# Routed tiles of a mixture-of-experts layer: the spread of gathered rows moves from ScalarE's queue to SyncE's, with new distances for gathers, lists and weights

## What is computed

```python
x = x + ffn(cond(x, cond_512, ...), router_w, e_bias, gate_w, up_w, down_w, ...)   # x: (8, 1024, 512)

def ffn(y):                       # 8192 tokens, C = 512, E = 64 experts, K = 8, H = 256, HS = 1024
    shared = silu(y @ sh_gate) * (y @ sh_up) @ sh_down
    topk_idx, w = route(y)        # 8 of 64 experts per token, in 4 of 8 groups
    order = argsort(topk_idx.reshape(-1))
    tok = order // K
    g, u = ragged_dot(y[tok], gate_w, sizes), ragged_dot(y[tok], up_w, sizes)
    o = ragged_dot(silu(g) * u, down_w, sizes) * w.reshape(-1)[order][:, None]
    return shared + zeros.at[tok].add(o)
```

## Time and profile before

| | us |
|---|---|
| median of 3 runs | 3974.17 (3964.74 to 3979.28) |
| profiled execution, its own device time | 3965.72 |
| its span | 3964.0 |
| TensorE busy in the span | 3733.3 (94%) |
| VectorE, ScalarE, GpSimd busy | 2235.7, 1495.3, 1946.4 |
| first gate/up matmul of the routed stage, from the span's start | 1470.6 |
| end of its last down matmul | 3949.9 |

### The profile page before, as it was taken

How to read it: one execution, slowest core, us unless ns; L and a number is a source line. 1 busy time by engine, 2 the same in 40 slices (tenths; PEclk the granted TensorE clock), 3 DMA queues, 4 the chain that set the end, 5 groups by cost and what they waited for, 6 DMA issues and landing times.

```text
span 3964.0 us, 91393 instructions
## 1 busy us (share of the span) xinstructions
PE 3733.3 (94%) x17024; PEld 3040.4 (77%) x17025; DVE 2235.7 (56%) x4612; ACT 1495.3 (38%) x3339; POOL 1946.4 (49%) x1601
## 2 busy tenths in 40 slices
PE   7999999999999959999999999999999999999987
PEld 5877877878787848878878878787878778777775
DVE  4655555555555645555555555555555555566554
ACT  3222222222222214444444444444444444444443
POOL 1453333333333425655556556555656555555554
PEclk9999999999999979999999999999999999999998
DMA  5121112112111228888889888988888898899887
GB/s 181 51 57 44 44 54 54 44 44 65 44 44 54 44 70 181 182 196 177 177 191 184 182 189 182 200 176 188 178 190 185 187 201 175 194 204 204 198 185 158
DMA packets 589051, 550.56 MB, mean 139 GB/s; under 512 B 133625, under 2 KB 443265, under 8 KB 588929
## 3 DMA queue, kind: packets, MB, share of 16 engines
q0 software_dynamic: 136112, 281.38, 36.5%
q10 hardware_dynamic: 291584, 140.58, 13.9%
q1 hardware_dynamic: 161234, 127.04, 11.7%
HBM read 229.07 MB, written 179.19 MB: 103 GB/s over the span
## 4 chain that ended last, share of the span: by engine, by line
PE 46%; DMA 7%; issue 4%; ACTq 3%; DVE 2%; SPq 1%; DVEq 1%; ACT 1%; POOLq 0%; POOL 0%
PE bank L1231 30%; PE bank L1249 14%; DMA x_split<-x_rows 4%; PE bank L1240 2%; ACTq L1341 2%; DMA raw_d<-in_L_ffn_down_w_dram 1%; DMA out_dram<-o_rows,to_row 1%; DVE w_dn_l L30 1%; DMA lists<-slot_list 1%; DMA x_rows<-y_rows,from_row 1%; DVE x_cols L1407 0%; ACTq L1074 0%; SPq L1074 0%; ACT x_h L1289 0%; DVE w_gu_l L30 0%
## 5 line engine op out<-in xcount | busy, mean ns | idle before, releaser
L1193 POOL DMA_INDIRECT out_dram<-o_rows,to_row x532 | 879.5, 1653 | 278.2 <-issue 230.0
L1177 POOL DMA_INDIRECT x_rows<-y_rows,from_row x539 | 543.9, 1009 | 840.6 <-DMA x_split<-x_rows 605.5
L428 POOL DMA_INDIRECT slot_list<-ent,pos x512 | 503.9, 984 | 862.7 <-PE bank L454 385.4
L1231 PE MATMUL bank<-w_gu_h,x_h 128*128 x2128 | 844.3, 397 | 86.1 <-DVE x_l L30 42.7
L1231 PE MATMUL bank<-w_gu_h,x_l 128*128 x2128 | 840.3, 395 | 0.0
L1231 PE MATMUL bank<-w_gu_l,x_h 128*128 x2128 | 839.7, 395 | 0.0
L1407 DVE STREAM_TRANSPOSE x_cols<-x_split 128x512 f32<-128x512 f32 x535 | 580.1, 1084 | 293.9 <-DMA x_split<-x_rows 293.2
L1414 DVE TENSOR_TENSOR e_hf<-bank,e_sg 128x256 f32<-128x256 f32 x532 | 225.2, 423 | 684.4 <-ACT e_sg L1295 366.2
L1231 PEld LDWEIGHTS bank<-w_gu_h,x_h 128*128 128x128 f32 x2128 | 406.4, 191 | 186.4 <-issue 99.1
L1249 PE MATMUL bank<-w_dn_h,e_h_h 128*128 x1064 | 468.1, 440 | 33.7 <-DVE e_h_l L30 20.5
L1231 PEld LDWEIGHTS bank<-w_gu_l,x_h 128*128 128x128 f32 x2128 | 406.9, 191 | 86.7
(11 more groups left out here) (242 smaller groups left out, 5946.7 us busy)
## 6 DMA issues: line engine op xcount, KB each, us to landing
x_split<-x_rows ACTq DMA_DIRECT2D x1072, 128.0 KB
xin<-in_x_dram SPq DMA_DIRECT2D x16, 1024.0 KB
y_rows<-yrow SPq DMA_DIRECT2D x64, 256.0 KB
stage_d<-in_x_dram SPq DMA_DIRECT2D x16, 1024.0 KB
out_dram<-stage_d SPq DMA_DIRECT2D x16, 1024.0 KB
raw_gu<-in_L_ffn_gate_w_dram SPq DMA_DIRECT2D x29, 512.0 KB
raw_gu<-in_L_ffn_up_w_dram SPq DMA_DIRECT2D x29, 512.0 KB
raw_d<-in_L_ffn_down_w_dram SPq DMA_DIRECT2D x29, 512.0 KB
```

What stands on the lines that cost most here:

```text
L428: nc.gpsimd.indirect_dma_start(slots, bass.IndirectOffsetOnAxis(ap=pos[v][:, t, k:k + 1], axis=0), ent[v][:, t, k, :], None).then_inc(scat ...
L1177: nc.gpsimd.indirect_dma_start(xg[u // 2][:, u % 2, :], None, y_rows, bass.IndirectOffsetOnAxis(ap=from_row[u][:].bitcast(U32), axis=0)).t ...
L1193: nc.gpsimd.indirect_dma_start(out, bass.IndirectOffsetOnAxis(ap=to_row[u][:].bitcast(U32), axis=0), og[u][:], None, compute_op=ALU.add).t ...
L1231: last = nc.tensor.matmul(b_gu[u % 2][:], xp[a][:, u % 2, k, :], wgu[b][:, bass.ds(place, 1), k, :].rearrange("p a n -> p (a n)"), start=( ...
```

## The change

The spread is issued by SyncE, in a new step there; ScalarE's `spread` is gone. SyncE's step j now is: list of tile j + 12, spread of the pair j + 6 and j + 7 if j is even, weights of tile j + 6. GpSimd's step gathers tile j + 8 instead of j + 7, and 8 instead of 7 gathers are issued ahead of the loop. VectorE's `rows_from` runs one tile further ahead. The number of buffers and all other orders stay. The list of tile j + 12 waits, as before, for the scatter of the tile 16 before it, which is tile j - 4. Beside it a few nops follow waits.

```diff
-            AHEAD = UN
+            LIST_AHEAD, SPREAD_AHEAD, LOAD_AHEAD = 12, 6, 6
@@ sync @@
                     if not known or j >= UN:
                         sp.wait_ge(list_ld[u], 16 * g)
+                        sp.nop(nofuse=True)
...
+                def spread(j, v, g):
+
+                    for u in (2 * v, 2 * v + 1):
+                        sp.wait_ge(x_ld[u], 16 * (g + 1))
+                        sp.nop(nofuse=True)
+                    if not isinstance(j, int) or j >= UN:
+                        sp.wait_ge(dve_turned, j - 2)
+                        sp.nop(nofuse=True)
+                    for a in range(QD):
+                        sp.dma_start(x_split[v][a * SQ:(a + 1) * SQ, :, :, :].rearrange("c i u e -> c (i u) e"),
+                                     xg[v][:, :, a * P:(a + 1) * P]).then_inc(x_moved[v], 16)
...
-                def step(g, u, is_first):
-                    n = g * UN + u
-                    load_list(n, u, g)
-                    weights(n - AHEAD, is_first)
+                def step(g, u, turn):
+                    j = g * UN + u
+                    load_list(j + LIST_AHEAD, (u + LIST_AHEAD) % UN, g + (u + LIST_AHEAD) // UN)
+                    if u % 2 == 0:
+                        spread(j + SPREAD_AHEAD, (u + SPREAD_AHEAD) % UN // 2, g + (u + SPREAD_AHEAD) // UN)
+                    weights(j + LOAD_AHEAD, turn.first(u + LOAD_AHEAD - UN))
...
+                spread(0, 0, 0)
                 for n in range(UN, 2 * UN):
                     load_list(n, n - UN, 1)
-                for n in range(1, UN):
+                    if n == UN + 1:
+                        spread(2, 1, 0)
+                for n in range(1, LOAD_AHEAD):
                     weights(n, field(sp, n, 3, 1))
-                for n in range(2 * UN, LISTS):
+                for n in range(2 * UN, LIST_AHEAD):
                     load_list(n, n % UN, n // UN)
-                    weights(n - AHEAD, field(sp, n - AHEAD, 3, 1))
+                spread(UN, 0, 1)
+                sp.wait_ge(words, 1)
+                for g in range(2):
+                    turn = Turn(sp, g + 1)
+                    for u in range(UN):
+                        step(g, u, turn)
                 last_turn = field(sp, 0, 5, NTURN - 1)
-                sp.wait_ge(words, 1)
-                with sp.Fori(LISTS // UN, NTURN + 2) as g:
-                    with sp.If(last_turn >= g - 2):
-                        turn = Turn(sp, g - 1)
+                with sp.Fori(2, NTURN) as g:
+                    with sp.If(last_turn >= g):
+                        turn = Turn(sp, g + 1)
                         for u in range(UN):
-                            step(g, u, turn.first(u))
+                            step(g, u, turn)
...
@@ gpsimd @@
-                    gather(g + 1 + (u + 3) // UN, (u + 3) % UN)
+                    gather(g + 2, u)
...
-                for n in range(UN + 3):
+                for n in range(2 * UN):
                     gather(n // UN, n % UN)
...
@@ scalar @@
-                def spread(j, v, g):
-
-                    for u in (2 * v, 2 * v + 1):
-                        act.wait_ge(x_ld[u], 16 * (g + 1))
-                        act.nop(nofuse=True)
...
-                    if u % 2 == 0:
-                        spread(j + UN, u // 2, g + 1)
-
-                spread(0, 0, 0)
-                spread(2, 1, 0)
@@ vector @@
-                    rows_from(j + 2 * UN, u, g + 2)
+                    rows_from(j + 2 * UN + 1, (u + 1) % UN, g + 2 + (u + 1) // UN)
...
+                rows_from(2 * UN, 0, 2)
```

More of the change, by code:

```diff
@@ L1150, in _ @@
                         weights(0, field(sp, 0, 3, 1))
+                spread(0, 0, 0)
                 for n in range(UN, 2 * UN):
                     load_list(n, n - UN, 1)
-                for n in range(1, UN):
+                    if n == UN + 1:
+                        spread(2, 1, 0)
+                for n in range(1, LOAD_AHEAD):
                     weights(n, field(sp, n, 3, 1))
-                for n in range(2 * UN, LISTS):
+                for n in range(2 * UN, LIST_AHEAD):
                     load_list(n, n % UN, n // UN)
-                    weights(n - AHEAD, field(sp, n - AHEAD, 3, 1))
+                spread(UN, 0, 1)
[4 more added lines that the diff above has]
+                        step(g, u, turn)
                 last_turn = field(sp, 0, 5, NTURN - 1)
-                sp.wait_ge(words, 1)
-                with sp.Fori(LISTS // UN, NTURN + 2) as g:
-                    with sp.If(last_turn >= g - 2):
-                        turn = Turn(sp, g - 1)
+                with sp.Fori(2, NTURN) as g:
+                    with sp.If(last_turn >= g):
+                        turn = Turn(sp, g + 1)
                         for u in range(UN):
-                            step(g, u, turn.first(u))
+                            step(g, u, turn)
                 for u in range(UN):
-                    sp.wait_ge(list_ld[u], 16 * last_turn + 48)
+                    sp.wait_ge(list_ld[u], 16 * last_turn + 16 * (1 + LIST_AHEAD // UN))
+                    sp.nop(nofuse=True)
+                for v in range(UN // 2):
+                    sp.wait_ge(x_moved[v], 16 * QD * last_turn + 16 * QD * (3 - v))
                     sp.nop(nofuse=True)
@@ L1216, in _ @@
                 for u in range(UN):
-                    pool.wait_ge(x_ld[u], 16 * last_turn + (48 if u < 3 else 32))
+                    pool.wait_ge(x_ld[u], 16 * last_turn + 48)
                 for u in range(UN):
```

## The result

The changed kernel takes 4357.96 us, median of 4 runs (4350.54 to 4362.6), against 3976.73 for the kernel before, median of 4 runs (3964.74 to 3986.67): ratio 1.0958 [1.0924, 1.0993], 381 us slower. Two more comparisons on other chips gave 1.0956 and 1.0969. The profiled execution took 4357.62 us for a span of 4355.9.

What follows compares the result with a forecast made beforehand. TensorE, busy 94% of the span, was taken as near the bound; after the change the cycle sets the pace: 2447 us plus 110 for loads, 2557 against 2479.3, +78; 3965.7 + 78 + 8.5 = 4052 us, range 3880 to 4180.

Steps and rivals of the forecast that it cites:

- the cycle: Four-tile loop of gather, scatter, SyncE's list, spread, next gather; forecast 18.4 us, 4.60 per tile, against TensorE's 4.33.
- A (the cycle fits): Rival: cycle below 17.3 us, TensorE keeps its pace, half of the 175 us return; 3887 us, chance 27%.
- B (no effect): Rival: SyncE reaches the spread no earlier than ScalarE did, and the cycle just fits; 3974 us, chance 11%.
- Gather to second scatter: Cycle term: GpSimd's own work from first gather to second scatter, start to start; 4.60 us.
- Scatter to the end of SyncE's wait: Cycle term: from the second scatter's start until SyncE's wait for it ends; 5.20 us, bounds 4.6 and 5.4.
- Wait to list: Cycle term on SyncE: end of the scatter wait to the list's DMA; 1.45 us, between 0.95 and 1.97.
- Spread to gather: Cycle term: a spread's first DMA to the gather it releases; 6.9 us, bounds 5.0 and 7.4.
- The 0.6 us that I took off for a lighter DMA load: Cycle deduction over spread and scatter, as a slower pace lightens the DMA engines from 0.88 to 0.80.
- the loads: 28 weight loads in the routed stage: 54 us for late close loads plus 56 for other costs, together 110.
- rival C: Rival: pace stays at 4.75 and spreads stand behind weights in SyncE's shared queue; 4173 us, chance 17%.
- those 175 us: Routed stage's 2479.3 us less 2304 at TensorE's pace; placed at weight loads, where spreads come late, 6.3 us each.
- L: Theory from the later experiments: lists late at weight loads are what is left; 50 to 100 us to regain.

Runs made afterwards that it cites:

- a2: The changed kernel with 32 buffers of lists instead of 16; 4036.58 us, ratio 1.0162 to the kernel before.
- a3: The changed kernel with GpSimd gathering tile j + 7 again, as before the change; 4058.62 us, ratio 1.0217 to the kernel before.
- a1: The changed kernel with the spread ahead of the list in SyncE's step; 4175.44 us, ratio 1.0511 to the kernel before.
- b3: The kernel before with four more unused register loads in each SyncE step; 4242.32 us, ratio 1.0729.
- c1: The kernel before with its spread issued one step earlier on ScalarE, five tiles ahead; 3999.61 us, ratio 1.0091.
- d2: The changed kernel unaltered, timed again in the third group; 4343.51 us, ratio 1.0956 to the kernel before.
- e1: The changed kernel unaltered, timed again in the fourth group; 4341.45 us, ratio 1.0969 to the kernel before.
- b4: The changed kernel with 32 buffers of lists and weights eight instead of six tiles ahead; 3866.53 us, ratio 0.9779 to the kernel before.
- e3: Same kernel as b4 (32 lists, weights eight ahead), timed again in the fourth group; 3989.32 us, ratio 1.0079 to the kernel before.
- e2: Same kernel as a2 (32 lists), timed again in the fourth group; 3988.53 us, ratio 1.0065 to the kernel before.
- b1: The changed kernel with spread ahead of the list, 32 lists and gather of tile j + 7; 3881.25 us, ratio 0.9816 to the kernel before.
- f1: Same as d1 but with lists 16 instead of 12 tiles ahead; 3875.32 us, ratio 0.9813 to the kernel before.
- f2: Same as e4 but with lists 16 instead of 12 tiles ahead; 3885.94 us, ratio 0.9832 to the kernel before.
- d1: The changed kernel with spread first, 32 lists, gather of tile j + 7 and weights eight ahead; 3981.55 us, ratio 1.0045 to the kernel before.
- e4: Same as d1, with half of each spread's DMAs issued by ScalarE; 3993.3 us, ratio 1.0097 to the kernel before.

## Why the prediction was wrong in size and right in kind

*Direction and mechanism: right.* The change is slower, the loss is in the routed stage, in quiet stretches too, and the cycle carries it: its turn can be read in the trace, and opening it (a2), shortening it by a gather and a scatter (a3), or taking the list out of it (a1) give back 321, 299 and 183 of the 381 us. The signs came in kind: VectorE waits for the spread 232 times for 266 pairs, and ScalarE for a load of weights 26 times, 136.7 us in all. TensorE's busy share in the quiet stretch fell further than forecast, to 106.36 / 120 = 0.89 instead of 0.94. Rivals A (the cycle fits) and B (no effect) are refuted by the time and by the quiet pace.

*The step that failed: the cycle's sum, taken as 18.4 us and measured as 21.0.* The quiet pace is 5.18 (the one stretch), not 4.60 us: 532 x 0.58 = 309 us, against a miss of 4358 - 4052 = 306. By terms, the medians of the 208 quiet turns:

- Gather to second scatter 4.75 for 4.60: right.
- Scatter to the end of SyncE's wait 6.3, where I had 5.20 and at most 5.4. This is the term that I mis-sized most. I had one value of it, 5.36. Where SyncE really waited the median is 6.3 too, so it is the scatter's own way to landing; for the same scatters of the kernel before (of even tiles) it is 5.5. Why it grew, although the DMA load fell, is open. In the 55 turns in which SyncE came late the mean is 7.6.
- Wait to list 1.0 for 1.45. I read the 1.97 of the earlier trace rows as the cost of a real wait. It holds one register instruction of 0.71 us, a long one of the kind that the last section shows; turns with and without a real wait have the same median.
- List to spread 0.8 for 0.85: right.
- Spread to gather 7.8, where I had 6.9 and at most 7.4. The issue saved nothing (0.67 each on either queue). The spread lands 7.0 us after its first issue, against 6.8 in the kernel before.
- The 0.6 us that I took off for a lighter DMA load did not come, though the load did fall to 0.77. That such waits grow fastest near full use no run shows.

*The range failed with it.* My upper bound of the cycle was 20.7 us. By my own sum that is 532 x 20.7 / 4 = 2753, with 110 for the loads 2863 us of stage, and 4358 us in all. The range ended at rival C's 4180, so I had not carried the bounds of the cycle into it. That this meets the measured time to the microsecond is luck, since the bounds of the single terms are not what was measured.

*What I never added up:* SyncE's own time. I laid spreads into its queue and costed only their distance. Its waits before, the two rows and 13.5 us more, leave 3.03 us of own time per tile, and 3.03 + 2.69 / 2 = 4.38 is more than TensorE's 4.33. In the changed kernel this is the smaller part: the 55 late turns cost 1.1 us each, or 0.3 us on the mean turn. It sets what the repairs can reach. b3 shows that SyncE's time by itself can bound this kernel, and a2, with 53 us of waits in the whole stage, that it was about full on that chip as soon as the cycle was open.

*"That is all that any change of order can give back"*, and the reading of those 175 us, was half right. I put them on late spreads at loads. c1 takes these waits away, and the tiles near loads lose nearly what they lost, 143 us against 151. So the waits at the earlier trace rows named the last to come, not the only one late.

*Rival C and the ring order.* Its time, 4173, was nearer, by another way. The Trainium skill, DMA: Bandwidth & Descriptors, Queues, rings and completion order, has it that each DMA engine consumes descriptors in ring order. From that I had worked out that spreads would stand behind weights in the shared queue, for 3.2 or 7.6 us. The traces price it. In the changed kernel a spread issued within 4 us after weights lands 8.3 us after its first issue (median of 10), other spreads 7.0: 1.3 us more. In the kernel before, from ScalarE's own queue, it is 12.0 (median of 16) against 6.8. So C's price is refuted: behind weights in the shared queue a spread landed sooner than beside them from another. Whether the order itself holds, no run here tests, and most of the loss is where no weights are in the queue.

*The loads:* 110 predicted. By the one stretch they cost 122, by all quiet tiles 80, and by the same count 54 and 46 in d2 and e1. So I had them too high rather than right. b4 and e3 show that the wait for weights can be taken away; e3, beside e2, gains nothing by it.

*What stays open:* why the kernels with the cycle open and one or more of the other repairs take 3867 to 3886 us on two chips (b1, b4, f1, f2) and 3982 to 3993 on two others (d1, e3, e4), and what bounds them at their loads. It is there that they differ: against 4.33 us per tile the tiles near a load lose 102 to 131 us in the first and 165 to 171 in the second, the quiet tiles at most 9 and 20 to 31. The kernel before and c1 belong to the picture: c1, with a SyncE that waits 1010 us, is about as slow as d1 and e4. So neither SyncE's total time nor the wait for weights is it; L is neither shown nor excluded.

## What to carry to other kernels

Before work is moved to a queue, write down each wait that the moved step will stand behind, and follow it until it returns or ends. Read each term of such a cycle over many turns and not from one row, and carry its bounds into the range. Then take the stage's length less the queue's waits, divide by the tiles, and add what is to be moved: where the sum comes near the pace, the queue will soon be the next bound. A buffer's reuse wait (here the list's, 16 tiles back) closes such loops, and more buffers open them. A large sum of waits for a transfer is no promise: take it away once, cheaply, before building on it.

## What the runs showed of the hardware

SyncE's instructions do not take the same time on all chips. The list's step from 2200 to 2600, of the same kernel (b4, then e3): ns min/median/max.

```profile
L1121 SPq MOVE lists<-slot_list x90: 29/29/38, 2200.0 to 2598.4; - x90
L1121 SPq DMA_DIRECT2D lists<-slot_list x90: 350/355/368, 2200.1 to 2598.5; - x90
```

```profile
L1121 SPq MOVE lists<-slot_list x86: 3/29/709, 2202.6 to 2595.4; - x86
L1121 SPq DMA_DIRECT2D lists<-slot_list x86: 5/350/710, 2202.7 to 2595.5; - x86
```

The medians agree; the second has a tail up to 0.7 us. Less its waits, SyncE needs (2421 - 220) / 532 = 4.14 us per tile in the first and (2518 - 56) / 532 = 4.63 in the second. The tail on this line is there in the profiles of the kernel before, of the changed one, and of the first, third and fourth groups; the second and fifth groups have none. (Register loads have outliers in both, up to 1205 ns in b3.) The chips differ elsewhere too: the routed stage begins 1422 to 1426 us after the span's start in the second and fifth groups and 1447 to 1476 in the other profiles, though the setup and the dense stage are the same in all. All kernels that beat the one before were timed on chips without the tail. That goes together on these chips; that the tail is the cause is not shown, since e4, with SyncE's time down to 4.15 us per tile despite it, is no faster. The kernel before hardly tells the chips apart: its medians are 3951 to 3977 us. No trace of it was kept from a chip without the tail. A gain of 2% on one chip was none on the next, so the version to keep (b1 or f1) would have to be timed on several.
